# A quantised gated MLP behind attention: the turn back of the scales, two roundings, a kept product and the last gate product moved, and the scale chains cut by one operation

## The chip, the cores and the metric

The kernel runs on one core of one Trainium2 chip. The metric is the device time of one execution in microseconds (us). The core has five engines that work side by side and meet at semaphores: PE (TensorE, matmul; its weight loads are listed apart as PEld), DVE (VectorE), ACT (ScalarE), POOL (GpSimd) and SP (SyncE, which here only issues DMAs). Every engine works through its own list of instructions in order, so an instruction that waits holds back all that stand behind it on that engine.

## The reference, cut to what matters

```python
x = x + tanh(g_xattn) * attention(layernorm(x), ctx, ctx)        # x: 16 x 128 x 512, float32
x = x + tanh(g_ffn)   * ffn(layernorm(x), w_gate, w_up, w_down)

def act_quant(x):                       # per token, 8 bit
    scale = 127.0 / clip(max(abs(x)), EPS)
    return clip(round(x * scale), -128, 127) / scale
def weight_quant(w):                    # ternary
    scale = clip(mean(abs(w)), EPS)
    return clip(round(w / scale), -1, 1) * scale
def h_bitlinear(x, w):
    return act_quant(fwht(x)) @ weight_quant(w).T
def ffn(h, wg, wu, wd):                 # H = 512, I = 2048
    return h_bitlinear(silu(h_bitlinear(h, wg)) * h_bitlinear(h, wu), wd)
```

`fwht` is the normalised Walsh-Hadamard transform along the last axis. Its factors are `C_E` = 512 to the power -1/2 and `C_I` = 2048 to the power -1/2; `QMAX` is 127.

## The kernel before, in words

Attention goes over 16 batches of 128 tokens first; PE sets its pace. The MLP then goes over 4 units (u = 0 to 3) of 4 batches (512 tokens) each. For a unit there are three stages on PE:

- **Gate and up** (`gate_up`): 16 blocks `ob`, each with a gate product (4 matmuls of 128x512 into banks 0 and 2 in turn) and an up product (4 matmuls into banks 1, 3 and 6 in turn). DVE scales the gate product (`gate`, L1391), ACT takes Silu of it (L1091), and DVE multiplies it with the up product (`hidden`, L1396). DVE does `gate(ob)` and then `hidden(ob - 1)`. `gs_done` counts gates, `h_done` hiddens, and PE waits on them before it writes a bank again.
- **Transform** (`transform`): 16 steps that turn the hidden values of the unit, each with 4 float32 matmuls against `had_f` (L863, two entries each in the profile), a copy by ACT (`y_high`), the low part by DVE (`low`, L1371), a second pair of matmuls (L875, L877) and a copy by ACT to `Z`. Between the steps the input of the next unit is normalised, transformed and quantised: `first_turn` (PE, L753), `first_had` (PE, L760), `input_peak` and `input_round` (DVE, L1334 to L1359), for each of its 4 batches tb. The normalised rows come from `front_statistics` (DVE) over `front_scales` (POOL, L517 to L522), `apply` (ACT, L1085) and `front` (POOL, L533 to L540); the rounded rows `q_b` are turned by a DMA into `q1_t`, which the next gate and up reads.
- **Down** (`project`): 4 blocks tb of 16 matmuls (L884). Block tb needs the DMA transposes of pieces 2 tb and 2 tb + 1 of the rounded `Z`, which SP issues in order (`turn`, L344).

The quantisation of a unit u runs beside the gate and up of unit u + 1. DVE takes the maxima of `Z` (`peak`, L1410); PE turns them (L842, after block 4); DVE works out the scales (`chain`, at ob 5, L1417 to L1429); PE turns those back and spreads them (`chain_back`, L849 and L851, after the up product of block 6); DVE copies them out (`chain_end`, at ob 7 behind `hidden(6)`, L1434 to L1438); POOL scales the 8 pieces of `Z` (`scale`, L555); ACT rounds pieces 0 and 1 (`rounding`, L1109 and L1111, after Silu 10 and Silu 12), and DVE the others (L1442): pieces 2, 3, 4 and 5 at ob 12, 13, 14 and 15, pieces 6 and 7 behind the gate and up.

Units 0 and 1 are quantised and projected so in a loop of two rounds: transform(u), gate_up(u + 1), project(u). Then come transform(2), gate_up(3), 11 of the 16 matmuls of the first down block of unit 2 (`project_kept(0, 0, AHEAD)`), transform(3) with no next input, the rest of the down product of unit 2 with the scale chain of unit 3 between its parts, and the down product of unit 3. `mz` is turned at L933 there.

Of the kernel before, what the change touches and what calls it, by code (L numbers as in the profile page):

```python
# [71 lines left out]
def flamingo_block(nc, x, k_t, v, w, gates, ident, had, had16, g_mask, g_mask_t, t_mask, out):  # L72
    with ExitStack() as ctx:
# [138 lines left out]
        AHEAD = 11  # L212
        LAST_PEAKS = {5: 0, 7: 1, 9: 2, 11: 3, 13: 4, 14: 5}
# [17 lines left out]
        ROUND_ACT = {10: 0, 12: 1}  # L231
# [138 lines left out]
        def _(pool):  # L370
# [197 lines left out]
        def _(pe):  # L568
# [238 lines left out]

            def gate_up(u, chain=None, first=False):
                for tb in range(UB):
                    reach(pe, sem(f"q1_in{tb}"), u.times(16, 16))  # L810
                for ob in range(NC):
                    if ob == 1:
                        reach(pe, sem("f_sg"), u.times(UB, UB))
                        if not first:
                            reach(pe, sem("f_su"), u.times(1, 1))
                    if first and ob == 1:
                        weigh(NB - 1, 1)
                        turn_out(NB - 1, 0)
# [9 lines left out]
                    for m, name, banks, used in ((0, "g_done", G_BANKS, "gs_done"), (1, "u_done", U_BANKS, "h_done")):  # L828
                        n = len(banks)
                        if ob >= n:  # L830
                            pe.wait_ge(sem(used), u.times(NC, ob + 1 - n))
                        elif chain is not None and banks[ob] > 5:
                            pe.wait_ge(sem("z_out"), chain.times(16, 16))
                        for j in range(NJ):
                            last = pe.matmul(ps[:, banks[ob % n], :], tern_gu[:, ob // 2, m, j, P * (ob % 2):P * (ob % 2) + P],  # L835
                                             q1_t[:, j, :], start=(j == 0), stop=(j == NJ - 1))
                        last.then_inc(sem(name), 1)
                    if chain is not None and ob == 4:
                        reach_apart(pe, sem("ones_set"),
                                    (sem("mz_done"), chain.times(8, 8)),  # L840
                                    (sem("y_low"), chain.times(16, 16)))
                        pe.transpose(ps[0:NG, 4, 0:P], mz[:, :], ident_f[:, :]).then_inc(sem("c_t1"), 1)  # L842
                    if chain is not None and ob == 6:
                        chain_back(chain)
# [10 lines left out]
            def transform(u, nxt):  # L855

                reach(pe, sem("h_done"), u.times(NC, NC))
                for s in range(18):
# [8 lines left out]
                    if s > 1:  # L867
# [4 lines left out]
                        elif z == 0:  # L872
# [56 lines left out]
            project_kept(0, AHEAD, NC)  # L929
# [240 lines left out]
        def _(dve):  # L1170
# [98 lines left out]
            def early_peak(tb):  # L1269

                dve.wait_ge(sem("f_hc"), tb + 1)
                dve.tensor_reduce(f_max[:, 0:1], had_out, AX_X, ALU.max, apply_absolute_value=True).then_inc(sem("f_c"), 1)
                dve.wait_ge(sem("f_c"), 5 * tb + 1)
                dve.tensor_scalar(f_max[:, 1:2], f_max[:, 0:1], C_E, EPS, ALU.mult, ALU.max).then_inc(sem("f_c"), 1)
                dve.wait_ge(sem("f_c"), 5 * tb + 2)
# [3 lines left out]
                dve.wait_ge(sem("f_c"), 5 * tb + 4)  # L1279
                dve.tensor_scalar(f_max[:, 3:4], f_max[:, 2:3], QMAX * C_E, None, ALU.mult).then_inc(sem("f_c"), 1)  # L1280

            def early_round(tb):

                dve.wait_ge(sem("f_c"), 5 * tb + 5)
                dve.tensor_scalar(q_int, had_out, f_max[:, 3:4], MAGIC, ALU.mult, ALU.add).then_inc(sem("f_qf"), 1)
# [48 lines left out]
            def input_peak(n, bank=1):  # L1334
# [4 lines left out]
                dve.wait_ge(sem("f_c"), n.times(5, 1))  # L1339
                dve.tensor_scalar(f_max[:, 1:2], f_max[:, 0:1], C_E, EPS, ALU.mult, ALU.max).then_inc(sem("f_c"), 1)  # L1340
                dve.wait_ge(sem("f_c"), n.times(5, 2))
                dve.reciprocal(f_max[:, 2:3], f_max[:, 1:2]).then_inc(sem("f_c"), 1)
                dve.tensor_scalar(f_max[:, 4:6], wsc[:, 0:2], f_max[:, 1:2], 1.0 / QMAX, ALU.mult, ALU.mult
                                  ).then_inc(sem("f_c"), 1)
                dve.wait_ge(sem("f_c"), n.times(5, 4))
                dve.tensor_scalar(f_max[:, 3:4], f_max[:, 2:3], QMAX * C_E, None, ALU.mult).then_inc(sem("f_c"), 1)
                dve.wait_ge(sem("f_c"), n.times(5, 5))
                dve.tensor_scalar(q_int, ps[:, bank, :], f_max[:, 3:4], MAGIC, ALU.mult, ALU.add
# [64 lines left out]
            def chain(u):  # L1413
# [52 lines left out]
            def gates_and_chain(u, prev, more=False):  # L1466
                reach(dve, sem("a2_done"), u.times(16))
                for ob in range(NC):
                    gate(u, ob)
                    if ob == 1 and prev is None:  # L1470
                        dve.wait_ge(sem("signed"), 12)
                    if ob > 0:
                        hidden(u, ob - 1)
# [11 lines left out]
                    else:  # L1485
# [4 lines left out]
                        if ob == 7:  # L1490
                            chain_end(prev)
# [117 lines left out]
```

## Time and profile before

| | |
|---|---|
| median of 3 runs | 481.35 us (481.11 to 481.57) |
| the profiled execution | 481.52 us |
| its span, first to last instruction | 479.7 us |
| granted TensorE clock, mean | 1.000 of full speed |
| PE busy | 462.8 us, 96% |
| DVE busy | 392.5 us, 82% |
| ACT busy | 292.8 us, 61% |
| POOL busy | 211.8 us, 44% |

Between the profiled execution and its span lie 1.8 us that are no engine's. A busy share is a mean over stages: a PE that is 96% busy can still wait at a few places, and an engine with a smaller share can be the one that sets a stage. Ends of matmuls are modelled: a matmul is shown with its latency, some 0.16 us beyond the time at which the next one could start.

### The profile page before, as it was taken

Reading aid. Unit: us, or ns where it says so; the run is one execution under the profiler, and the core shown is the slowest. Engines: PE = TensorE matmul, PEld = TensorE weight load, DVE = VectorE, ACT = ScalarE, POOL = GpSimd, SP = SyncE. Lnnn points to the kernel's source line nnn. Section 1 sums busy time; section 2 is a strip of 40 time slices with the busy share of each in tenths; the row PEclk is TensorE's granted clock in tenths of the full one; section 3 lists DMA queues with packets and bytes.
Section 4 is the critical chain, followed back from the end, with each engine's and each line's share of the span. In section 5 each row is a group of like instructions: output and inputs, shape, how many; then the busy total and the mean of one; then the engine's idle time right before and its main releaser. Section 6 shows DMA issues by size and latency. Waiting matters only on the chain.

```text
span 479.7 us, 9075 instructions
## 1 busy us (share of the span) xinstructions
PE 462.8 (96%) x3130; PEld 299.9 (63%) x3130; DVE 392.5 (82%) x765; ACT 292.8 (61%) x465; POOL 211.8 (44%) x314
## 2 busy tenths in 40 slices
PE   8999999999999999989999999999999999989997
PEld 7665656665666434468844479854468874469664
DVE  4889988798968749859997967998885999879892
ACT  3578886677768668877645517653616653648470
POOL 4245455978987544654005834201936200840000
PEclk9999999999999999999999999999999999999999
DMA  6999220021022023000100550100371110153086
GB/s 195 305 348 338 81 53 15 20 57 25 13 66 78 12 56 132 1 1 13 23 11 3 109 138 27 22 11 0 61 158 44 24 23 0 22 88 69 0 134 218
DMA packets 68183, 35.90 MB, mean 75 GB/s; under 512 B 50288, under 2 KB 62960, under 8 KB 68144
## 3 DMA queue, kind: packets, MB, share of 16 engines
q1 hardware_dynamic: 67728, 34.61, 28.2%
q10 hardware_dynamic: 416, 0.79, 0.5%
q8 instruction: 22, 0.36, 0.3%
q14 instruction: 17, 0.14, 0.1%
HBM read 19.26 MB, written 4.19 MB: 49 GB/s over the span
## 4 chain that ended last, share of the span: by engine, by line
PE 63%; DVE 20%; issue 7%; DMA 5%; ACT 3%; SPq 1%; DVEq 0%
PE ps L835 11%; PE ps L884 9%; PE ps L610 9%; PE ps L593 9%; PE ps L636 6%; PE ps L863 5%; DVE y_split L1371 4%; PE ps L653 4%; DVE mz L1410 3%; DVE wst L1391 3%; DMA reg_rest<-reg 2%; PE ps L618 2%; DVE f_max L1337 2%; DVE wst L1396 2%; PE ps L690 1%
## 5 line engine op out<-in xcount | busy, mean ns | idle before, releaser
L835 PE MATMUL ps<-wst 128*128 128x512 bf16 x512 | 112.5, 379 | 0.5 <-DMA wst<-q_b 0.5
L1224 DVE TENSOR_REDUCE reg<-ps 128x4 f32<-128x512 f32 x128 | 82.0, 685 | 25.1 <-PE ps L610 24.3
L555 POOL TENSOR_TENSOR reg_rest<-reg_rest,z_sc 128x1024 f32<-128x1024 f32 x24 | 48.2, 2045 | 92.0 <-DVE z_sc L1434 92.0
L959 ACT ACTIVATE reg<-ps 128x1024 f32<-128x1024 f32 x64 | 65.5, 1023 | 35.7 <-PE ps L618 35.3
L610 PE MATMUL ps<-reg 32*128 32x256 f32 x512 | 86.7, 400 | 0.5 <-DVE reg L1224 0.3
L835 PEld LDWEIGHTS ps<-wst 128*128 128x128 bf16 x512 | 49.5, 98 | 59.6 <-issue 1.8
L593 PE MATMUL ps<-reg 32*128 32x512 f32 x256 | 71.9, 639 | 0.0
L1091 ACT ACTIVATE wst<-wst 128x512 f32<-128x512 f32 x64 | 40.0, 626 | 51.9 <-DVE wst L1391 51.5
L863 PE MATMUL ps<-had_f,wst 128*128 128x128 f32 x512 | 67.1, 275 | 1.3 <-DVE wst L1396 1.3
L863 PEld LDWEIGHTS ps<-had_f,wst 128*128 128x128 f32 x512 | 64.1, 191 | 4.4 <-DVE wst L1396 1.8
L610 PEld LDWEIGHTS ps<-reg 32*128 32x128 f32 x512 | 58.6, 184 | 5.7 <-issue 1.1
L1121 ACT CAST y_split<-ps 128x512 fp32r<-128x512 f32 x64 | 37.3, 586 | 39.6 <-PE ps L863 39.6
L1371 DVE TENSOR_TENSOR y_split<-ps,y_split 128x512 fp32r<-128x512 f32 x64 | 43.5, 684 | 15.0 <-ACT y_split L1121 15.0
L1391 DVE TENSOR_TENSOR wst<-ps,wst 128x512 f32<-128x512 f32 x64 | 43.7, 682 | 10.4 <-PE ps L835 10.4
L884 PE MATMUL ps<-wst,reg_rest 128*128 128x512 bf16 x192 | 42.6, 380 | 3.5 <-DMA reg_rest<-reg 3.5
L1396 DVE TENSOR_TENSOR wst<-ps,wst 128x512 f32<-128x512 f32 x64 | 43.5, 679 | 1.0 <-ACT wst L1091 0.8
L450 POOL TENSOR_TENSOR x_all<-x_all,reg 128x256 f32<-128x256 f32 x32 | 23.8, 745 | 35.8 <-DVE reg L1237 35.8
L1130 ACT COPY reg_rest<-ps 128x512 f32<-128x512 f32 x64 | 37.8, 592 | 2.2 <-PE ps L877 2.1
L884 PEld LDWEIGHTS ps<-wst,reg_rest 128*128 128x128 bf16 x192 | 27.2, 144 | 18.1 <-DMA reg_rest<-reg 2.7
L1410 DVE TENSOR_REDUCE mz<-reg_rest 128x8 f32<-128x1024 f32 (+1 forms) x33 | 38.3, 1171 | 0.0
L636 PE MATMUL ps<-reg 128*32 128x512 f32 x256 | 34.1, 605 | 0.0
L593 PEld LDWEIGHTS ps<-reg 32*128 32x128 f32 x256 | 19.2, 183 | 22.5 <-issue 21.0
(167 smaller groups left out, 747.4 us busy)
## 6 DMA issues: line engine op xcount, KB each, us to landing
wst<-in_w SPq DMA_DIRECT2D x16, 512.0 KB, 8.2
reg<-in_w SPq DMA_DIRECT2D x8, 512.0 KB, 5.4
out<-x_all SPq DMA_DIRECT2D x16, 256.0 KB, 2.1
x_all<-in_x SPq DMA_DIRECT2D x3, 1024.0 KB, 9.9
reg<-in_k_t SPq DMA_DIRECT2D x32, 32.0 KB, 2.3
reg<-in_v SPq DMA_DIRECT2D x4, 256.0 KB, 3.5
x_all<-in_x ACTq DMA_DIRECT2D x1, 512.0 KB, 4.3
reg_rest<-reg SPq DMA_TRANSPOSE x20, 3.2
```

The source lines that it names most:

```text
L593: pe.matmul(ps[:, bank + m, :], kpad[b // CHUNK % 2][strip(i), b % CHUNK, a, :], q_t[b % 4][strip(i), :], start=True, stop=False)
L610: last = pe.matmul(ps[:, row_banks(r) + m, 256 * g:256 * g + 256], q_t[n % 4][strip(i), P * h:P * h + P], kpad[n // CHUNK % 2][strip(i), n ...
L636: last = pe.matmul(O_BANK[SLOT * l:SLOT * l + SLOT, :], v_pad[n // CHUNK % 2][:, n % CHUNK, 4 * kvh + l, :], probs[:, 4 * kvh + l, :], sta ...
L835: last = pe.matmul(ps[:, banks[ob % n], :], tern_gu[:, ob // 2, m, j, P * (ob % 2):P * (ob % 2) + P], q1_t[:, j, :], start=(j == 0), stop= ...
L863: last = pe.matmul(ps[:, Y_BANKS[s % 3], P * k:P * k + P], X[:, 4 * s + k, :, :].rearrange("p c t -> p (c t)"), had_f[:, :], start=True, s ...
L884: last = pe.matmul(ps[:, bank, :], q2.rearrange("p g (t c) -> p c (g t)", c=NC)[:, c, P * tb:P * tb + P], tern_d[:, c, :], start=(c == 0), ...
L959: act.activation(probs[:, 2 * j:2 * j + 2, :], ps[:, bank:bank + 2, :], ACT.Exp, scale=D ** -0.5).then_inc(sem("exp_done"), 1)
L1224: dve.tensor_reduce(neg_max[n % 2][:, g:g + 2, i + m, :], ps[:, row_banks(r) + m, :].rearrange("p (g a t) -> p g a t", g=2, a=2), AX_X, AL ...
L1371: dve.tensor_tensor(y_low[s % RING], ps[:, Y_BANKS[s % 3], :], y_high[s % RING].bitcast(F32), ALU.subtract).then_inc(sem("y_low"), 1)
L1391: dve.tensor_tensor(gs[ob % GS], ps[:, G_BANKS[ob % 2], :], s_row, ALU.mult).then_inc(sem("gs_done"), 1)
L1396: dve.tensor_tensor(X[:, :, ob, :], ps[:, U_BANKS[ob % 3], :].rearrange("p (g t) -> p g t", g=NG), gs[ob % GS].rearrange("p (g t) -> p g t ...
L1410: dve.tensor_reduce(mz[:, g0:g1], Z[:, g0:g1, :], AX_X, ALU.max, apply_absolute_value=True).then_inc(sem("mz_done"), 1)
```

## The change

- In `gate_up` the 8 matmuls of a block are split into a helper `rows`. `chain_back` moves from behind the up product of block 6 to between the gate and the up product of block 7. The gate product of block 15 moves ahead of the up product of block 14: gate 14, gate 15, up 14, up 15. This holds for all four units (`chain_back` for three).
- On DVE `chain_end` moves from behind `hidden(6)` to ahead of it, at ob 7.
- ACT rounds pieces 0 and 1 after Silu 9 and 11 instead of after Silu 10 and 12.
- The input's scale chain (`early_peak`, `input_peak`) loses its last multiplication (L1280, L1346): the factor 1/127 goes into the maximum's scaling, so the reciprocal is the rounding's factor itself. The unit's scale chain (`chain`) loses one too (L1427 and L1429 become one TENSOR_TENSOR with two broadcast operands). The counts of `f_c` and `c_step` go from 5 to 4.
- In the last transform the last 5 matmuls of the first kept down block are issued at step z = 14, between the second matmuls of z = 14 and of z = 15, instead of behind the transform.

```diff
+        KEPT_FILL = {14: (11, 16)}
-        ROUND_ACT = {10: 0, 12: 1}
+        ROUND_ACT = {9: 0, 11: 1}
...
+            def rows(u, chain, ob, m, name, banks, used):
+                n = len(banks)
+                if ob >= n:
+                    pe.wait_ge(sem(used), u.times(NC, ob + 1 - n))
+                elif chain is not None and banks[ob] > 5:
+                    pe.wait_ge(sem("z_out"), chain.times(16, 16))
+                for j in range(NJ):
+                    last = pe.matmul(ps[:, banks[ob % n], :], tern_gu[:, ob // 2, m, j, P * (ob % 2):P * (ob % 2) + P],
+                                     q1_t[:, j, :], start=(j == 0), stop=(j == NJ - 1))
+                last.then_inc(sem(name), 1)
...
+                    if ob < NC - 1:
+                        rows(u, chain, ob, 0, "g_done", G_BANKS, "gs_done")
+                    if chain is not None and ob == 7:
+                        chain_back(chain)
+                    if ob == NC - 2:
+                        rows(u, chain, NC - 1, 0, "g_done", G_BANKS, "gs_done")
+                    rows(u, chain, ob, 1, "u_done", U_BANKS, "h_done")
...
-                    if chain is not None and ob == 6:
-                        chain_back(chain)
...
+                        if nxt is None and z in KEPT_FILL:
+                            project_kept(0, *KEPT_FILL[z])
...
             transform(last_u, None)
-            project_kept(0, AHEAD, NC)
             project_kept(1, 0, 3)
...
-                dve.tensor_scalar(f_max[:, 1:2], f_max[:, 0:1], C_E, EPS, ALU.mult, ALU.max).then_inc(sem("f_c"), 1)
+                dve.tensor_scalar(f_max[:, 1:2], f_max[:, 0:1], 1.0 / QMAX, EPS / (QMAX * C_E), ALU.mult, ALU.max).then_inc(sem("f_c"), 1)
...
-                dve.tensor_scalar(f_max[:, 4:6], wsc[:, 0:2], f_max[:, 1:2], 1.0 / QMAX, ALU.mult, ALU.mult
+                dve.tensor_scalar(f_max[:, 4:6], wsc[:, 0:2], f_max[:, 1:2], C_E, ALU.mult, ALU.mult
                                   ).then_inc(sem("f_c"), 1)
-                dve.wait_ge(sem("f_c"), n.times(5, 4))
-                dve.tensor_scalar(f_max[:, 3:4], f_max[:, 2:3], QMAX * C_E, None, ALU.mult).then_inc(sem("f_c"), 1)
-                dve.wait_ge(sem("f_c"), n.times(5, 5))
-                dve.tensor_scalar(q_int, ps[:, bank, :], f_max[:, 3:4], MAGIC, ALU.mult, ALU.add
+                dve.wait_ge(sem("f_c"), n.times(4, 4))
+                dve.tensor_scalar(q_int, ps[:, bank, :], f_max[:, 2:3], MAGIC, ALU.mult, ALU.add
...
-                dve.tensor_tensor(cz[:, 5, :], cz[:, 3, :], su[:, 1, :], ALU.mult).then_inc(c, 1)
-                dve.wait_ge(c, u.times(5, 5))
-                dve.tensor_scalar(q_sc[:, :, :], cz[:, 5, :].unsqueeze(2).broadcast_to([NG, T8, NC]), QMAX * C_I, None,
-                                  ALU.mult).then_inc(sem("c_qs"), 1)
+                dve.tensor_tensor(q_sc[:, :, :], cz[:, 3, :].unsqueeze(2).broadcast_to([NG, T8, NC]),
+                                  su[:, 1, :].unsqueeze(2).broadcast_to([NG, T8, NC]), ALU.mult).then_inc(sem("c_qs"), 1)
...
                     gate(u, ob)
+                    if prev is not None and ob == 7:
+                        chain_end(prev)
                     if ob > 0:
                         hidden(u, ob - 1)
...
-                        if ob == 7:
-                            chain_end(prev)
```

## Rows read from the trace of the kernel before

**Rows 1.** The page, part 1: busy time and share of each engine.
```profile
PE 462.8 (96%) x3130; PEld 299.9 (63%) x3130; DVE 392.5 (82%) x765; ACT 292.8 (61%) x465; POOL 211.8 (44%) x314
```

**Rows 2.** Who waited for whom: us in total, times, longest.
```profile
PE ps L884 <- DMA reg_rest<-reg: 3.5, 3, 1.7
PE ps L849 <- DVE diag L1429: 1.5, 3, 0.5
```

**Rows 3.** Timeline around `chain_back` in gate_up(1): start, duration, instruction, [idle before].
```profile
252.72 1.03 PE L835 MATMUL ps<-wst 128*128 128x512 bf16 x4
...
253.88 0.22 DVE L1429 TENSOR_SCALAR diag<-cz 64x128 f32<-64x128 f32 x1
254.25 0.24 PE L849 MATMUL ps<-ident_f,diag 64*128 64x64 f32 x1 [0.51 <-DVE diag L1429]
...
257.85 16.23 POOL L555 TENSOR_TENSOR reg_rest<-reg_rest,z_sc 128x1024 f32<-128x1024 f32 x8 [30.65 <-DVE z_sc L1434]
```

**Rows 4.** Timeline of ACT, then the chain that ended last, into project(0).
```profile
262.79 1.13 ACT L1109 ACTIVATE reg_rest<-reg_rest,magics 128x1024 f32<-128x1024 f32 x1
...
267.41 1.16 ACT reg L1111
...
268.58 3.23 DMA reg_rest<-reg
...
271.85 14.04 PE ps L884 x64
```

**Rows 5.** Timeline of DVE, blocks 13 to 15 of gate_up(1) and behind.
```profile
267.63 0.68 DVE L1391 TENSOR_TENSOR wst<-ps,wst 128x512 f32<-128x512 f32 x1
...
273.43 1.19 DVE L1442 TENSOR_SCALAR reg<-reg_rest 128x1024 bf16<-128x1024 f32 x1
...
275.14 1.28 DVE L1442 TENSOR_SCALAR reg<-reg_rest 128x1024 bf16<-128x1024 f32 x2
```

**Rows 6.** Timeline of the next unit's first normalised batch, beside project(0).
```profile
280.75 0.15 DVE L1191 TENSOR_SCALAR ve<-mv 128x1 f32<-128x1 f32 x1
...
285.70 0.73 POOL L540 TENSOR_TENSOR scratch4k<-wst 128x256 f32<-128x256 f32 x1
...
286.62 0.60 PE L753 MATMUL ps<-ident_f,scratch4k 128*128 128x128 f32 x4
```

**Rows 7.** Busy time by stretch, in transform(1).
```profile
298.00:317.00 19.00, 18.29 (x130) 15.75 (x129) 18.54 (x42) 12.93 (x28) 2.84 (x4) 1.00 0.10 21
```

**Rows 8.** Timeline of DVE and POOL, input batches 0 and 3 in transform(1).
```profile
293.75 0.15 DVE L1346 TENSOR_SCALAR f_max<-f_max 128x1 f32<-128x1 f32 x1
...
293.93 0.75 DVE L1348 TENSOR_SCALAR wst<-ps,f_max 128x512 f32<-128x512 f32 x1
...
295.55 0.72 POOL L539 TENSOR_TENSOR scratch4k<-wst 128x256 f32<-128x256 f32 x1 [0.16 <-POOL wst L534]
295.60 0.76 DVE L1358 TENSOR_SCALAR diag<-ident_f,f_max 128x128 f32<-128x128 f32 x1
...
314.37 0.28 DVE L1358 TENSOR_SCALAR diag<-ident_f,f_max 128x128 f32<-128x128 f32 x1
```

**Rows 9.** Timeline at the end of gate_up(0).
```profile
207.43 1.13 ACT L997 ACTIVATE wst<-reg,magics 128x1024 bf16<-128x1024 f32 x1
...
210.03 1.16 PE L863 MATMUL ps<-had_f,wst 128*128 128x128 f32 x8 [1.31 <-DVE wst L1396]
```

**Rows 10.** The chain that ended last and the timeline, end of gate_up(3).
```profile
419.73 3.98 DMA reg_rest<-reg
...
422.88 1.47 DVE L1396 TENSOR_TENSOR wst<-ps,wst 128x512 f32<-128x512 f32 x2
...
423.85 2.57 PE L884 MATMUL ps<-wst,reg_rest 128*128 128x512 bf16 x11 [1.72 <-DMA reg_rest<-reg]
```

**Rows 11.** Timeline at the end of transform(3).
```profile
448.76 0.50 PE L875 MATMUL ps<-y_split,had_r 128*128 128x512 f32 x1 [0.99 <-DVE y_split L1371]
...
451.07 0.11 PEld L933 LDWEIGHTS ps<-ident_f,mz 128*64 128x64 f32 x1 [0.23 <-DVE mz L1410]
```

More of the change, by code:

```diff
@@ L470, in early_scales @@
             def early_scales(tb):
-                pool.wait_ge(sem("f_c"), 5 * tb + 5)
+                pool.wait_ge(sem("f_c"), 4 * tb + 4)
                 reach(pool, sem("f_t2"), tb)
@@ L827, in gate_up @@
                         pe.wait_ge(sem("signed"), ob + 2)
[L828 to L837, printed above, removed]
+                    if ob < NC - 1:
[5 more added lines that the diff above has]
+                    rows(u, chain, ob, 1, "u_done", U_BANKS, "h_done")
                     if chain is not None and ob == 4:
@@ L1272, in early_peak @@
                 dve.tensor_reduce(f_max[:, 0:1], had_out, AX_X, ALU.max, apply_absolute_value=True).then_inc(sem("f_c"), 1)
-                dve.wait_ge(sem("f_c"), 5 * tb + 1)
-                dve.tensor_scalar(f_max[:, 1:2], f_max[:, 0:1], C_E, EPS, ALU.mult, ALU.max).then_inc(sem("f_c"), 1)
-                dve.wait_ge(sem("f_c"), 5 * tb + 2)
+                dve.wait_ge(sem("f_c"), 4 * tb + 1)
+                dve.tensor_scalar(f_max[:, 1:2], f_max[:, 0:1], 1.0 / QMAX, EPS / (QMAX * C_E), ALU.mult, ALU.max).then_inc(sem("f_c"), 1)
+                dve.wait_ge(sem("f_c"), 4 * tb + 2)
                 dve.reciprocal(f_max[:, 2:3], f_max[:, 1:2]).then_inc(sem("f_c"), 1)
-                dve.tensor_scalar(f_max[:, 4:6], wsc[:, 0:2], f_max[:, 1:2], 1.0 / QMAX, ALU.mult, ALU.mult
+                dve.tensor_scalar(f_max[:, 4:6], wsc[:, 0:2], f_max[:, 1:2], C_E, ALU.mult, ALU.mult
                                   ).then_inc(sem("f_c"), 1)
-                dve.wait_ge(sem("f_c"), 5 * tb + 4)
-                dve.tensor_scalar(f_max[:, 3:4], f_max[:, 2:3], QMAX * C_E, None, ALU.mult).then_inc(sem("f_c"), 1)
             def early_round(tb):
-                dve.wait_ge(sem("f_c"), 5 * tb + 5)
-                dve.tensor_scalar(q_int, had_out, f_max[:, 3:4], MAGIC, ALU.mult, ALU.add).then_inc(sem("f_qf"), 1)
+                dve.wait_ge(sem("f_c"), 4 * tb + 4)
+                dve.tensor_scalar(q_int, had_out, f_max[:, 2:3], MAGIC, ALU.mult, ALU.add).then_inc(sem("f_qf"), 1)
             def early_integers(tb):
@@ L1338, in input_peak @@
                                   ).then_inc(sem("f_c"), 1)
-                dve.wait_ge(sem("f_c"), n.times(5, 1))
-                dve.tensor_scalar(f_max[:, 1:2], f_max[:, 0:1], C_E, EPS, ALU.mult, ALU.max).then_inc(sem("f_c"), 1)
-                dve.wait_ge(sem("f_c"), n.times(5, 2))
+                dve.wait_ge(sem("f_c"), n.times(4, 1))
+                dve.tensor_scalar(f_max[:, 1:2], f_max[:, 0:1], 1.0 / QMAX, EPS / (QMAX * C_E), ALU.mult, ALU.max).then_inc(sem("f_c"), 1)
+                dve.wait_ge(sem("f_c"), n.times(4, 2))
                 dve.reciprocal(f_max[:, 2:3], f_max[:, 1:2]).then_inc(sem("f_c"), 1)
-                dve.tensor_scalar(f_max[:, 4:6], wsc[:, 0:2], f_max[:, 1:2], 1.0 / QMAX, ALU.mult, ALU.mult
+                dve.tensor_scalar(f_max[:, 4:6], wsc[:, 0:2], f_max[:, 1:2], C_E, ALU.mult, ALU.mult
                                   ).then_inc(sem("f_c"), 1)
-                dve.wait_ge(sem("f_c"), n.times(5, 4))
-                dve.tensor_scalar(f_max[:, 3:4], f_max[:, 2:3], QMAX * C_E, None, ALU.mult).then_inc(sem("f_c"), 1)
-                dve.wait_ge(sem("f_c"), n.times(5, 5))
-                dve.tensor_scalar(q_int, ps[:, bank, :], f_max[:, 3:4], MAGIC, ALU.mult, ALU.add
+                dve.wait_ge(sem("f_c"), n.times(4, 4))
+                dve.tensor_scalar(q_int, ps[:, bank, :], f_max[:, 2:3], MAGIC, ALU.mult, ALU.add
                                   ).then_inc(sem("f_qf"), 1)
@@ L1418, in chain @@
                                   ).then_inc(c, 1)
-                dve.wait_ge(c, u.times(5, 1))
+                dve.wait_ge(c, u.times(4, 1))
                 dve.tensor_tensor(cz[:, 1, :], cz[:, 0, :], su[:, 1, :], ALU.mult).then_inc(c, 1)
-                dve.wait_ge(c, u.times(5, 2))
-                dve.tensor_scalar(cz[:, 2, :], cz[:, 1, :], C_I, EPS, ALU.mult, ALU.max).then_inc(c, 1)
-                dve.wait_ge(c, u.times(5, 3))
+                dve.wait_ge(c, u.times(4, 2))
+                dve.tensor_scalar(cz[:, 2, :], cz[:, 1, :], 1.0 / QMAX, EPS / (QMAX * C_I), ALU.mult, ALU.max).then_inc(c, 1)
+                dve.wait_ge(c, u.times(4, 3))
                 dve.reciprocal(cz[:, 3, :], cz[:, 2, :]).then_inc(c, 1)
-                dve.tensor_scalar(cz[:, 4, :], cz[:, 2, :], wsd_tg[0:NG, :], None, ALU.mult).then_inc(sem("c_qs"), 1)
-                dve.wait_ge(c, u.times(5, 4))
-                dve.tensor_tensor(cz[:, 5, :], cz[:, 3, :], su[:, 1, :], ALU.mult).then_inc(c, 1)
-                dve.wait_ge(c, u.times(5, 5))
-                dve.tensor_scalar(q_sc[:, :, :], cz[:, 5, :].unsqueeze(2).broadcast_to([NG, T8, NC]), QMAX * C_I, None,
-                                  ALU.mult).then_inc(sem("c_qs"), 1)
+                dve.tensor_scalar(cz[:, 4, :], cz[:, 2, :], wsd_tg[0:NG, :], QMAX * C_I, ALU.mult, ALU.mult
+                                  ).then_inc(sem("c_qs"), 1)
+                dve.wait_ge(c, u.times(4, 4))
+                dve.tensor_tensor(q_sc[:, :, :], cz[:, 3, :].unsqueeze(2).broadcast_to([NG, T8, NC]),
+                                  su[:, 1, :].unsqueeze(2).broadcast_to([NG, T8, NC]), ALU.mult).then_inc(sem("c_qs"), 1)
             def chain_end(u, f_tok=f_tok):
```

## The prediction

> **What bounds the kernel now.** I read the page's shares first: PE is busy 96% of the span, so what can be won is PE's idle time and whatever makes a stage longer than PE's own work [rows 1]. The list of waits says where PE stood idle for others: three times for the DMA that turns the rounded values, in front of a down product, 3.5 us in all (one of 1.7, two of 0.9), and three times 0.5 us for the scales that `chain_back` turns [rows 2]. Then I went through the timeline stage by stage. Attention is PE work on both sides and the change touches nothing on its path. Gate and up is PE-bound except at `chain_back`. A transform with a next input is DVE's: between 298 and 317 us DVE is busy 18.54 of 19 us, and PE's matmuls wait in small pieces for it [rows 7]. Transform(3) is PE's, with a tail that DVE sets.
>
> **chain_back between gate 7 and up 7.** The last 4 matmuls of up 6 start at 252.72, follow each other at 0.22 us (64 down matmuls take 14.04 us) and leave PE free at 253.58; the turn back starts at 254.25, right behind DVE's last chain operation, done at 254.10 [rows 3, 4]. So PE loses 0.67 us (0.51 in the list, which counts from the modelled end). With gate 7 (4 x 0.22 = 0.87 us) in front, PE comes to the turn back at 254.45, after the scales. Cost 0, gain 0.67 in each of three units. No row shows the new TENSOR_TENSOR with two broadcast operands over 128 elements: below it cannot be under the 0.22 of the operation that it replaces, above it is under the 0.74 of an L1396 with 512 elements [rows 3, 10]. I take about 0.3, nearer to the 0.22 since it has the same 128 elements. One operation of 0.18 less stands in front of it, so the scales come at about 254.0, or at 254.45 by the upper end: both are in time for PE.
>
> `chain_end` no longer waits behind `hidden(6)`. The spread scales are ready about 1.1 us of `chain_back` after 254.45, and DVE is then just past `gate(7)`. I put the copy at 255.65 and POOL's first block at 255.85 instead of 257.85, 2.0 us earlier; it ends its 16.2 us at 272.1 instead of 274.1 [rows 3].
>
> **Roundings after Silu 9 and 11.** PE's down product waits for piece 1: rounded by ACT until 268.57, landed 3.23 us later, PE starts at 271.85, 1.03 us after it could (0.87 in the list) [rows 4]. One block of gate and up is 8 x 0.22 = 1.73 us. With the pair of roundings (1.13 + 1.16 us) one block earlier and PE's 0.67 us, piece 1 is done about 2.3 us earlier, at 266.3, and lands at 269.5; PE is ready at 270.15. POOL's second block is done by 260, so the roundings don't wait for it. Silu 10 stands behind the first rounding and ends 0.2 us after `hidden(10)` would like it; DVE has 0.4 us to spare in each block there. The wait goes entirely: 1.03 us in each loop round.
>
> What is late next? Pieces 2 to 7 are rounded by DVE, which runs without a gap from block 12 on, and moves by PE's 0.67 only. Piece 5 is the tightest: rounded from 273.43 for 1.19 us beside POOL, while pieces 6 and 7, with POOL done, take 0.64 each [rows 5]. New, POOL ends at 272.1 and piece 5 starts at 272.8, so it should take 0.65 and end at 273.4, landing at 276.7; block 2 of the down product wants it at 270.15 + 32 x 0.22 = 277.1. In time by 0.4.
>
> But PE is then 1.70 us early at `first_turn`, and its rows come over another path: statistics on DVE (end 280.90), POOL, ACT, POOL's L540 (end 286.43), against PE's L753 at 286.62 [rows 6]. That path moves by DVE's 0.67 + 0.53 and has about 0.1 to spare. So PE waits 0.4 us at L753, and a loop round brings 1.3 us, not 1.7. Two rounds: 2.6 us.
>
> **Gate 15 ahead of up 14.** In gate_up(0), transform(0) waits 1.31 us for the last hidden [rows 9]. Gate 15 comes 0.87 us earlier, but ACT stands in front of Silu 15 with a weight sign operation from 207.43 to 208.56, and Silu 15 started at 208.62 already. Gain 0.1; if ACT were free it would be 0.5. In the other units PE now wants bank 2 at 268.2 in old time, and `gate(13)` frees it at 268.31 [rows 5]: a wait of 0.1, which in the loop is lost in the wait at L753.
>
> **The last unit.** The same 0.67, and PE's wait for piece 1 is 1.72 us, 1.88 from the last possible start; the landing took 3.98 us there [rows 10]. New it lands at 417.3 + 3.98 = 421.3, just when PE is ready. The 11 matmuls then end 2.5 us earlier. Transform(3) also needs `hidden(15)`, done at 424.35 in old time and 0.67 earlier now, 423.7, against PE at 423.8. Gain 2.4 us, which passes whole through the PE-bound transform(3).
>
> **Shorter input chain.** L1346 to L1348 is 0.18 us from start to start [rows 8], 12 times in the three DVE-bound transforms: 2.2 us if all of it counts. For input batches 0 and 1 I count nothing: DVE's next scalar operations run beside POOL's four operations of the following batch and end with them, L1358 takes 0.76 us against POOL's L539, and 0.28 where POOL is idle [rows 8]. POOL's times come from PE's `first_turn` and don't move with the chain. Batches 2 and 3 have no such neighbour: 2 x 0.18 = 0.4 a transform, 1.1 us in all, and the ends are 0 and 2.2. The Trainium skill (SBUF — State Buffer, "Who interferes with whom") says that a two-port tensor_scalar on DVE and a GpSimd operation exclude each other for the whole instruction; by that rule batches 0 and 1 give 0, and the trace agrees with L1358's 0.76 against 0.28 us. The same section speaks against the new TENSOR_TENSOR, whose two SBUF inputs would wait behind a reading POOL; here POOL has been idle for 30.65 us, so it costs nothing.
>
> **Kept product into transform(3).** Between the second matmuls of z = 14 and z = 15 PE has a hole of 1.2 us (0.99 in the list) before 448.76; 5 x 0.22 = 1.1 fill it. What follows is L933 at 451.07, which waits for DVE's maxima, not for PE [rows 11]. The time that the 5 matmuls leave behind becomes idle in front of L933. Gain 0, loss at most 1.1. The shorter unit chain brings nothing there either, since 9 kept matmuls lie between the two turns.
>
> **Sum.** 0.1 + 2.6 + 1.1 + 2.4 = 6.2 us from the 481.5 of the profiled execution, 475.3; the median of the runs is 0.15 lower, so 475.2.
>
> **Rivals.**
> - The input chain counts in full: DVE is nearly always busy in these transforms, but the neighbouring POOL work speaks against it. 1.1 us more, 474.1. Chance 0.14.
> - The input chain counts for nothing, because the DMA turn of `q_b` or ACT sets the end of the transform: 476.3. Against it stands DVE's saturation. Chance 0.10.
> - Piece 5 stays at 1.19 us beside POOL. Then the statistics move 0.53 less and PE waits that much longer at L753, twice: 476.3; with a landing of 3.98 instead of 3.23 us block 2 of the down product waits as well and it is 476.9. Chance 0.15. The rule of the Trainium skill on the shared port (SBUF — State Buffer, "Who interferes with whom") is on the other side: with POOL done before piece 5 starts, nothing holds it.
> - No change within 0.2%: the waits at the down product all come back at the next pieces, L753 and the last unit's `hidden(15)`, and only the turn back remains, under 1 us. Chance 0.03.
> - Slower: the roundings, now in front of Silu 10 and 11, hold `hidden(10)` and with it `gate(12)`, `gate(13)` and PE at gate 15, where the order of this change leaves no slack. The whole pair (2.3 us) passed on, less DVE's 0.4 of spare time, is 1.9 us, twice in three units, 11.4 us against 6.2: 486.7. It decides from 1.0 us per rounding on. Before the change the same two roundings stood in front of Silu 11 and 13 and held nothing. Chance 0.02.
>
> The forecast itself has 0.56, with 474.6 to 476.0 as its own range. The bounds of the terms (0 to 0.5; 1.3 to 3.4; 0 to 2.2; 0.7 to 2.5) would reach from 472.8 to 479.5; I cut to 473.6 to 477.2. A difference under 0.2% (1 us) is about what a measurement can't tell from none. Faster 0.95, same 0.03, slower 0.02.
>
> **What would show it.** L849 with no idle before it, three times; POOL's L555 some 2 us earlier against PE's L849; the first L884 of each down product directly behind L835; L753 with an idle of about 0.4 behind project; L1442 of piece 5 at 0.65 us; L863 still waiting over 1 us after gate_up(0); idle in front of L933 longer, the stretch from L933 to the end unchanged at 28.6 us. The prediction is wrong if PE waits at gate 15, or at later blocks of the down product.

## The result and the profile after

| | median | range | runs |
|---|---|---|---|
| before | 481.46 us | 481.11 to 481.59 | 4 |
| after | 476.32 us | 475.92 to 476.53 | 4 |

The ratio is 0.9893 (95% interval 0.9878 to 0.9909), 5.1 us faster. The forecast was 475.2 us, made of 6.2 us of gain. The profiled execution of after took 475.92 us, its span is 474.1 us, the granted TensorE clock 1.000.

The page of after, part 1, and below it the list of waits (us in total, times, longest):

```profile
PE 459.7 (97%) x3110; PEld 299.1 (63%) x3130; DVE 390.8 (82%) x745; ACT 293.0 (62%) x465; POOL 211.3 (45%) x314
```

```profile
PE ps L817 <- DVE wst L1396: 2.1, 3, 0.7
PE ps L761 <- DVE wst L1353: 1.2, 3, 0.4
PE ps L871 <- DVE wst L1401: 1.1, 1, 1.1
PE ps L942 <- DVE mz L1415: 0.9, 1, 0.9
...
PE ps L754 <- POOL scratch4k L541: 0.2, 1, 0.2
```

Both entries of [rows 2] are gone: no DMA wait in front of a down product, none in front of the turn back (L857 now). In their place a new one stands on top: L817 is the gate and up product, L1396 is `gate`. Three times 0.7 us, once in each of the units 1 to 3, PE waits for a gate product's bank. The forecast had 0.1 there.

The timeline of after in gate_up(1), start, duration, instruction, [idle before], the same stretch as [rows 3, 4, 5]; L556 is `scale` on POOL, L1446 `rounding` on DVE, L894 the down product:

```profile
252.22 0.28 DVE L1433 TENSOR_TENSOR diag<-cz,su 64x128 f32<-64x128 f32 x1
...
252.87 0.27 PE L857 MATMUL ps<-ident_f,diag 64*128 64x64 f32 x1
...
254.51 15.78 POOL L556 TENSOR_TENSOR reg_rest<-reg_rest,z_sc 128x1024 f32<-128x1024 f32 x8 [28.22 <-DVE z_sc L1438]
...
263.78 1.89 POOL L556 TENSOR_TENSOR reg_rest<-reg_rest,z_sc 128x1024 f32<-128x1024 f32 x1
...
263.97 2.26 DVE L1446 TENSOR_SCALAR reg<-reg_rest 128x1024 bf16<-128x1024 f32 x1
266.15 0.68 DVE L1396 TENSOR_TENSOR wst<-ps,wst 128x512 f32<-128x512 f32 x1
...
266.88 2.76 PE L817 MATMUL ps<-wst 128*128 128x512 bf16 x12 [0.70 <-DVE wst L1396]
267.35 1.18 DVE L1446 TENSOR_SCALAR reg<-reg_rest 128x1024 bf16<-128x1024 f32 x1
...
269.48 6.86 PE L894 MATMUL ps<-wst,reg_rest 128*128 128x512 bf16 x30
...
271.95 0.68 DVE L1446 TENSOR_SCALAR reg<-reg_rest 128x1024 bf16<-128x1024 f32 x1
```

Read it from below. PE's idle of 0.70 us ends with `gate(13)`, which DVE starts at 266.15 because piece 2's rounding held it for 2.26 us. That rounding starts 0.19 us behind the start of a POOL block. Up to there the blocks follow each other at 1.86 us; the next one starts at 265.64, and 1.67 us of waiting and 0.6 of work make the 2.26. Before, the same rounding had started 1.01 us into its block and took 1.44, a row that the forecast never looked at. These two rows of before show it:

```profile
265.26 1.89 POOL L555 TENSOR_TENSOR reg_rest<-reg_rest,z_sc 128x1024 f32<-128x1024 f32 x1
...
266.27 1.44 DVE L1442 TENSOR_SCALAR reg<-reg_rest 128x1024 bf16<-128x1024 f32 x1
```

Where the 5.6 us between the two spans come from, by the start of the same instruction on both sides. For the transforms the mark at their end is DVE's first `gate`, since PE's first row there can lack a matmul record (0.21 us).

| stage | measured | forecast |
|---|---|---|
| launch to the third batch of attention | -0.34 | not counted; 55.00 to 56.05 us in the 14 profiled kernels |
| attention from there (input chain of unit 0) | -0.61 | 0 |
| gate_up(0) | -0.13 | -0.1 |
| three transforms with a next input (0.40, 0.45, 0.47) | -1.32 | -1.1 |
| two loop rounds of gate and up and down (0.57, 0.66) | -1.23 | -2.6 |
| gate_up(3) to the end | -1.96 | -2.4 |

The rest of the rows that answer to those of before, all from the timeline of after: the end of gate_up(0) [rows 9], the next unit's first turn [rows 6], input batch 0 in transform(1) [rows 8], the end of gate_up(3) [rows 10], and the end of transform(3) [rows 11].

```profile
206.52 1.13 ACT L1006 ACTIVATE wst<-reg,magics 128x1024 bf16<-128x1024 f32 x1
...
208.95 1.16 PE L871 MATMUL ps<-had_f,wst 128*128 128x128 f32 x8 [1.14 <-DVE wst L1401]
...
284.57 0.65 PE L754 MATMUL ps<-ident_f,scratch4k 128*128 128x128 f32 x4 [0.22 <-POOL scratch4k L541]
...
291.49 0.21 DVE L1350 TENSOR_SCALAR f_max<-wsc,f_max 128x2 f32<-128x2 f32 x1
...
291.74 0.75 DVE L1353 TENSOR_SCALAR wst<-ps,f_max 128x512 f32<-128x512 f32 x1
...
412.95 2.26 DVE L1446 TENSOR_SCALAR reg<-reg_rest 128x1024 bf16<-128x1024 f32 x1
...
415.87 2.76 PE L817 MATMUL ps<-wst 128*128 128x512 bf16 x12 [0.70 <-DVE wst L1396]
...
418.47 2.54 PE L894 MATMUL ps<-wst,reg_rest 128*128 128x512 bf16 x11
...
442.50 1.03 PE L894 MATMUL ps<-wst,reg_rest 128*128 128x512 bf16 x4
...
443.37 0.50 PE L883 MATMUL ps<-y_split,had_r 128*128 128x512 f32 x1
...
445.68 0.30 PE L942 MATMUL ps<-ident_f,mz 128*64 128x128 f32 x1 [0.87 <-DVE mz L1415]
```

The operation between L1350 and L1353 is gone. In unit 3 the 11 kept matmuls follow without the 1.72 us for the DMA, but behind the same 0.70 at gate 15. Transform(3) has kept matmuls in its hole (four of the five have a record) and pays in front of L942 (0.87 us of idle, 0.23 in [rows 11]); and from there to the end it is 28.4 us, 28.6 before.

### The profile page after: what moved, and what is told of

Read it like the earlier page. It is cut to its first block, busy times and chain, and to the rows that moved or that the text cites. A ratio compares the mean times of both kernels' runs of the same rounds, so it can differ in the third digit from the quotient of the medians.

```text
span 474.1 us, 8995 instructions
## 1 busy us (share of the span) xinstructions
PE 459.7 (97%) x3110; PEld 299.1 (63%) x3130; DVE 390.8 (82%) x745; ACT 293.0 (62%) x465; POOL 211.3 (45%) x314
## 4 chain that ended last, share of the span: by engine, by line
PE 73%; DVE 13%; issue 7%; ACT 3%; POOL 2%; DMA 1%; DVEq 0%; POOLq 0%; ACTq 0%
PE ps L817 14%; PE ps L611 10%; PE ps L594 9%; PE ps L871 9%; PE ps L637 7%; PE ps L894 6%; PE ps L654 4%; PE ps L883 2%; PE ps L885 2%; PE ps L761 2%; DVE wst L1401 2%; PE ps L619 2%; PE ps L691 2%; DVE y_split L1376 2%; DVE st L1196 1%
## 5 line engine op out<-in xcount | busy, mean ns | idle before, releaser
L817 PE MATMUL ps<-wst 128*128 128x512 bf16 x499 | 111.7, 379 | 3.3 <-DVE wst L1396 2.1
L817 PEld LDWEIGHTS ps<-wst 128*128 128x128 bf16 x512 | 49.1, 98 | 62.1 <-DVE wst L1396 4.2
L556 POOL TENSOR_TENSOR reg_rest<-reg_rest,z_sc 128x1024 f32<-128x1024 f32 x24 | 47.3, 2009 | 84.7 <-DVE z_sc L1438 84.7
L1396 DVE TENSOR_TENSOR wst<-ps,wst 128x512 f32<-128x512 f32 x64 | 43.5, 680 | 8.2 <-PE ps L817 8.2
L894 PE MATMUL ps<-wst,reg_rest 128*128 128x512 bf16 x186 | 42.2, 380 | 0.4
L894 PEld LDWEIGHTS ps<-wst,reg_rest 128*128 128x128 bf16 x192 | 27.4, 145 | 13.9 <-issue 0.6
```

The lines of the kernel that those rows point to most:

```text
L556: pool.tensor_tensor(z, z, sc, ALU.mult).then_inc(sem("z_scaled"), 1)
L894: last = pe.matmul(ps[:, bank, :], q2.rearrange("p g (t c) -> p c (g t)", c=NC)[:, c, P * tb:P * tb + P], tern_d[:, c, :], start=(c == 0), ...
L1396: dve.tensor_tensor(gs[ob % GS], ps[:, G_BANKS[ob % 2], :], s_row, ALU.mult).then_inc(sem("gs_done"), 1)
```

## The experiments

All ran beside the kernel before (medians 481.35 to 481.62 in the four groups). The times below are medians with their ratio to it; after's own is 476.32 (0.9893). The edits are made in the kernel after.

**The input chains long again.**

```diff
-                dve.tensor_scalar(f_max[:, 1:2], f_max[:, 0:1], 1.0 / QMAX, EPS / (QMAX * C_E), ALU.mult, ALU.max).then_inc(sem("f_c"), 1)
+                dve.tensor_scalar(f_max[:, 1:2], f_max[:, 0:1], C_E, EPS, ALU.mult, ALU.max).then_inc(sem("f_c"), 1)
...
+                dve.tensor_scalar(f_max[:, 3:4], f_max[:, 2:3], QMAX * C_E, None, ALU.mult).then_inc(sem("f_c"), 1)
```

> The changed kernel with the fifth operation of the input's scale chain back, in attention (4 times) and in the three transforms (12 times). Reading of the two traces: attention lengthens by 0.14 us a batch, 0.55 us, each transform by 0.4 us, 1.2 us together: 477.9 to 478.3 us. Rival (the difference of the attention stages is that of two executions): 477.3 to 477.6 us. If all 12 count: 479.0 us.

478.80 us (478.60 to 479.03), 0.9943 [0.9929, 0.9956]: 2.5 us more than after. By the marks used above, attention from its third batch gives back 0.60 us, and the three transforms 0.40, 0.41 and 0.51; they are then as long as before's within 0.04. So the chain is worth 1.3 us in the transforms, the size that the forecast gave it, and 0.6 in attention, which it had put at nothing: four operations of 0.18 us are 0.72. The other 0.5 us of the 2.5 lies in neither. In the profiled execution the launch is 0.47 us longer than after's, and gate_up(3) to the end 0.69 (0.30 of it a wait for a DMA in the last down product); that these have to do with the chain is not shown.

**Gate 15 ahead in unit 0 only.**

```diff
-                    if ob < NC - 1:
+                    if ob < NC - 1 or not first:
                         rows(u, chain, ob, 0, "g_done", G_BANKS, "gs_done")
...
-                    if ob == NC - 2:
+                    if ob == NC - 2 and first:
```

> The changed kernel with gate 15 ahead of up 14 in the first unit only. In the changed kernel PE waits 0.70 us at gate 15 in each of units 1 to 3. Theory A (shared port: DVE rounds piece 2 in 2.26 us because it waits out a POOL block that began 0.19 us before it, and gate(13) comes late): these three waits go, since the old order wants gate(13) 0.87 us later; DVE's own times stay (2.26 us), so in the loop the 0.7 us is mostly lost again at the next first_turn, and only the last unit keeps it: 475.3 to 475.9 us. Theory B (gate 15 ahead is harmless, the time went elsewhere): 476.3 us, no change.

476.44 us (476.27 to 476.56), 0.9895 [0.988, 0.991]: no change, a miss for the expectation of 475.3 to 475.9. The order of the two products decides where PE waits, not how long the kernel takes. Piece 2 takes 2.27 us as in after; PE no longer waits at gate 15, but for what that lateness reaches next. Timeline of this kernel, round 1 and unit 3:

```profile
264.18 2.27 DVE L1446 TENSOR_SCALAR reg<-reg_rest 128x1024 bf16<-128x1024 f32 x1
...
276.13 7.12 PE L894 MATMUL ps<-wst,reg_rest 128*128 128x512 bf16 x31 [0.22 <-DMA reg_rest<-reg]
...
284.80 0.65 PE L754 MATMUL ps<-ident_f,scratch4k 128*128 128x128 f32 x4 [0.66 <-POOL scratch4k L541]
...
418.47 2.59 PE L894 MATMUL ps<-wst,reg_rest 128*128 128x512 bf16 x11 [0.40 <-DVE wst L1396]
```

**The two roundings of ACT back behind Silu 10 and 12.**

```diff
-        ROUND_ACT = {9: 0, 11: 1}
+        ROUND_ACT = {10: 0, 12: 1}
```

> The changed kernel with ACT's roundings after Silu 10 and 12 again. Theory A (shared port): piece 2 on DVE still takes about 2.26 us and PE still waits 0.7 us at gate 15, because POOL and DVE stand to each other as before; the down product waits for piece 1 by about 0.1 us in the loop and 0.9 us in the last unit, 477.0 to 477.6 us. Rival C (the moved roundings hold Silu 10 and 11 and so DVE and gate 15): piece 2 falls back to 1.4 us and the waits at gate 15 go; what is lost at piece 1 is won there, 476.0 to 476.6 us.

476.87 us (476.67 to 477.67), 0.9907 [0.9892, 0.9922]. Piece 2 takes 2.18 us and PE's waits at gate 15 stay, so the moved roundings don't make them:

```profile
264.44 2.18 DVE L1446 TENSOR_SCALAR reg<-reg_rest 128x1024 bf16<-128x1024 f32 x1
...
267.28 2.76 PE L817 MATMUL ps<-wst 128*128 128x512 bf16 x12 [0.71 <-DVE wst L1396]
```

A loop round is as long as after's, 43.23 us: with DVE late, the earlier piece 1 is worth nothing in the loop. In the last unit it is worth 0.26 us, the time by which transform(3) now starts later against the unit's first `gate`. Another 0.27 us lies behind the turn of `mz`, where nothing was changed and the kernels' profiles differ by up to 0.4 us among themselves (28.42 to 28.80).

**The turn back in its old place.**

```diff
-                    if chain is not None and ob == 7:
-                        chain_back(chain)
...
+                    if chain is not None and ob == 6:
+                        chain_back(chain)
```

> The changed kernel with the turn back behind up 6 again (the copy of the scales stays ahead of hidden 6). Theory A (shared port): PE loses 0.6 us at the turn back in three units again, but POOL's blocks begin about 1.4 us later against DVE, piece 2 then waits only 0.3 us for the port and takes about 1.0 us, and the three waits of 0.7 us at gate 15 go: 475.9 to 476.8 us, nearly no change. Rival D (the turn back's move simply gives 0.67 us a unit and the port has nothing to do with it): 478.3 us.

475.96 us (475.79 to 476.05), 0.9885 [0.987, 0.99]: no slower than after, a little faster if anything. The waits of [rows 2] in front of the turn back are back (0.57, 0.58, 0.56 us at L857); but POOL's first block now starts 14.31 us behind the unit's first `gate` instead of 13.17, the rounding 23.24 instead of 22.63, piece 2 takes 0.93 us, and no wait is left at gate 15. What one move gives, the other takes.

**POOL 0.6 us later, by the copy behind hidden(6) again.** The turn back stays in its new place.

```diff
-                    if prev is not None and ob == 7:
-                        chain_end(prev)
                     if ob > 0:
                         hidden(u, ob - 1)
+                    if prev is not None and ob == 7:
+                        chain_end(prev)
```

> The changed kernel with DVE's copy of the scales behind hidden(6) again: everything that depends on it, POOL's eight blocks first, begins 0.6 us LATER. Theory A (shared port): piece 2's rounding then meets the end of a POOL block after 0.45 us instead of 1.67 us and takes about 1.05 us instead of 2.26; the 0.7 us waits at gate 15 go; 473.6 to 474.6 us, faster by about 2 us. Rival E (an earlier start of POOL is a gain or nothing): 476.3 to 477.0 us.

474.97 us (474.38 to 475.52), 0.9869 [0.9854, 0.9884], 1.35 us faster than after. Nothing is done sooner here, one copy is done later:

```profile
255.84 16.24 POOL L556 TENSOR_TENSOR reg_rest<-reg_rest,z_sc 128x1024 f32<-128x1024 f32 x8 [28.80 <-DVE z_sc L1438]
264.72 0.99 DVE L1446 TENSOR_SCALAR reg<-reg_rest 128x1024 bf16<-128x1024 f32 x1
```

The rounding starts 8.88 us behind POOL's first block, 0.40 before the sixth starts (5 x 1.855 = 9.28), and takes 0.40 + 0.6. The list of waits has no L817 for L1396.

**The same aim by moving DVE's operation.** Piece 2 is rounded ahead of `hidden(11)` instead of behind it.

```diff
+                    if prev is not None and ob == 12:
+                        rounding(prev, 2)
                     if ob > 0:
                         hidden(u, ob - 1)
...
-                    if 12 <= ob < 14:
+                    if ob == 13:
```

> The changed kernel with DVE's rounding of piece 2 ahead of hidden(11) instead of behind it, 0.6 us earlier against POOL, whose start stays. Theory A (shared port): it waits 0.4 us and takes about 1.0 us; the waits at gate 15 go; 473.6 to 474.6 us. Rival E (DVE has the same work in either order): 476.3 us.

473.99 us (473.03 to 474.59), 0.9842 [0.9829, 0.9855]: 2.3 us under after. POOL keeps its early start and piece 2 takes 0.99 us. The last experiment below comes to the same time, with useless work in it; the loop rounds are the shortest here. So of all versions this is the one to keep.

**ACT rounds piece 2 as well** (after Silu 13), and DVE one less.

```diff
-        ROUND_ACT = {9: 0, 11: 1}
+        ROUND_ACT = {9: 0, 11: 1, 13: 2}
...
-                        if 12 <= ob < 14:
+                        if ob == 13:
```

> The changed kernel with piece 2 rounded by ACT (behind Silu 13) instead of DVE, POOL's start as in the changed kernel. Theory A (shared port): gate(13) follows hidden(11) at once and PE never waits at gate 15; piece 3, DVE's first, meets POOL instead and may wait up to a block, but behind gate(13), where PE has slack: 474.3 to 475.5 us. Rival (ACT, with three roundings, holds Silu 14 and 15): 476.3 us or slower.

475.55 us (475.34 to 475.57), 0.9871 [0.9853, 0.9888]. The wait at gate 15 is gone and a loop round is 0.4 us shorter than after's, but piece 3 now starts just behind the start of the seventh block and takes 2.31 us. ACT ends piece 2 at 268.51, DVE piece 3 at 268.53; SP issues their transposes one behind the other, at 268.54 and 269.81, the second lands at 273.16, and the down product waits for it:

```profile
266.22 2.31 DVE L1446 TENSOR_SCALAR reg<-reg_rest 128x1024 bf16<-128x1024 f32 x1
...
273.20 3.03 PE L894 MATMUL ps<-wst,reg_rest 128*128 128x512 bf16 x13 [0.54 <-DMA reg_rest<-reg]
```

**No kept matmuls in transform(3).**

```diff
-                        if nxt is None and z in KEPT_FILL:
+                        if False:
...
+            project_kept(0, AHEAD, NC)
```

> The changed kernel with the 5 kept matmuls behind transform(3) again. Both readings of the tail: what follows waits for DVE's maxima, so 476.3 us, no change; L942 then stands behind 8 matmuls instead of 3 and waits under 0.1 us instead of 0.87. If the fill had cost or brought its 1.1 us, 475.2 or 477.4 us.

476.59 us (476.50 to 476.60), 0.9898 [0.9883, 0.9913]. The hole before L883 is back (0.99 us), the wait in front of the turn of `mz` is gone, and gate_up(3) to the end is 0.18 us longer than after's, 0.11 of it ahead of the turn of `mz`: the fill is worth 0.1 to 0.2 us.

**POOL later by idle work of its own.** Three additions of 64x2 elements on POOL (0.49 us in all, into a row that nobody reads; their results are unused in this kernel and the next three) between POOL's wait for the scales and its first block.

```diff
                 reach(pool, sem("c_sc"), u.times(1, 1))
+                for k in range(3):
+                    pool.tensor_tensor(cz[:, 5, 2 * k:2 * k + 2], ones_f[0:NG, 0:2], ones_f[0:NG, 2:4], ALU.add).then_inc(sem("spare_done"), 1)
```

> The changed kernel with three added small POOL operations (64x2 elements each, results unused) between POOL's wait for the scales and its first block, on three units: 0.4 to 0.7 us of useless work that delays POOL and touches nothing else. Theory A (shared port): piece 2 takes 0.9 to 1.2 us instead of 2.26, the waits at gate 15 go, 473.6 to 474.6 us. Rival E: 476.3 us or slower.

494.29 us (493.70 to 495.08), 1.0265 [1.0251, 1.0279]. A miss by 20 us: the theory that only the phase counts (where in a POOL block DVE's operation starts) is not enough. Its timeline (`gate` is L1398 here, the rounding L1448, `scale` L558), and its busy time by stretch (length, PE, PEld, DVE, ACT, POOL busy with counts, granted clock, DMA share, GB/s):

```profile
262.69 7.45 POOL L558 TENSOR_TENSOR reg_rest<-reg_rest,z_sc 128x1024 f32<-128x1024 f32 x4
...
264.30 6.40 DVE L1448 TENSOR_SCALAR reg<-reg_rest 128x1024 bf16<-128x1024 f32 x1
...
271.35 4.87 PE L819 MATMUL ps<-wst 128*128 128x512 bf16 x11 [4.84 <-DVE wst L1398]
```

```profile
265.00:271.30 6.30, 1.51 (x7) 0.49 (x5) 6.30 (x3) 0.46 (x1) 5.14 (x3) 0.89 0.22 42
271.30:276.00 4.70, 4.65 (x11) 1.64 (x12) 4.54 (x8) 1.89 (x3) 0.00 (x0) 0.50 0.69 133
```

DVE doesn't come in at the end of the running block. POOL's last four go through back to back, 4 x 1.86 = 7.45 us, to 270.14, and only then does the rounding do its 0.6. PE idles 4.84 us; after that the granted clock is 0.50 over 4.7 us, the 1.2 GHz level, and a matmul takes 0.43 us instead of 0.22. Three times 4.84 against three times 0.70 us of wait are 12.4 of the 18 us that it costs against after. The rest, 5.6, is of the size of the halved clock: behind the three idles PE works on at 0.50 for 5.35, 2.80 and 5.08 us, and half of that, 6.6 us, is an upper estimate of its cost.

**Two, and five, such operations** (the five of 64x1 elements), to tell the phase from the operations themselves.

> The changed kernel with two added small POOL operations in place of the three of the run before, which made piece 2 take 6.40 us. POOL starts 0.3 us later than in the changed kernel, and a POOL block ends about 0.1 us after DVE comes to piece 2 (0.25 us with three). Plain lock (DVE gets the port at the next block's end): piece 2 takes 0.7 us, 473 to 474 us. If a DVE operation that comes shortly before a block's end misses it and then all that follow: about 6.5 us again, 493 to 496 us. If it is the presence of added operations: 6.4 us as well, which the run with five tells apart.

> The same with five added small POOL operations: a POOL block ends about 0.55 us after DVE comes to piece 2. If the place in time decides: piece 2 takes 1.15 us, no wait at gate 15, 474.0 to 475.2 us, although POOL does more and starts later than in the run at 494 us. If the presence of added operations decides: 6 us, about 494 us.

494.36 us (494.13 to 494.66), 1.0261 [1.0242, 1.0279], and 496.00 us (495.64 to 496.23), 1.0294 [1.0275, 1.0312]. Piece 2 takes 6.26 and 6.69 us, again until POOL's last block is done. With two, three and five operations the rounding starts 9.16, 9.03 and 8.74 us behind POOL's first block: three phases, one picture, so it is not the phase.

**The three operations with a wait for them** ahead of the first block.

```diff
+                reach(pool, sem("spare_done"), u.times(3, 3))
```

> The changed kernel with the three added small POOL operations that led to 494 us, and behind them a wait of POOL for their own completion, so that the first of the eight blocks follows a wait again, as in the changed kernel. If DVE is shut out because the blocks stand in POOL's queue behind operations without a wait: piece 2 takes 0.7 to 1.2 us and the time is 473.6 to 475.0 us. If the added operations as such (or POOL's code) decide: piece 2 takes over 6 us and the time is 493 to 495 us.

474.04 us (473.94 to 474.72), 0.9846 [0.983, 0.9863]. Timeline:

```profile
254.92 0.49 POOL L554 TENSOR_TENSOR cz<-ones_f 64x2 f32<-64x2 f32 x3 [28.22 <-DVE z_sc L1441]
255.48 16.24 POOL L559 TENSOR_TENSOR reg_rest<-reg_rest,z_sc 128x1024 f32<-128x1024 f32 x8
...
264.38 0.97 DVE L1449 TENSOR_SCALAR reg<-reg_rest 128x1024 bf16<-128x1024 f32 x1
```

The same useless half microsecond, and the kernel is 2.3 us faster than after instead of 18 us slower: with the wait in front, DVE gets in at the end of a block again, and the later phase pays. The rounding starts 8.90 us behind the first block, between the 8.74 and the 9.03 at which it was shut out, so the wait makes the difference and not the place in time.

## Why the prediction was nearly right, and what it missed

The start of the first rounding that DVE does beside POOL (piece 2; piece 3 where ACT takes piece 2), counted from the start of POOL's first block in gate_up(1), sorts the kernels whose first block directly follows a wait. Blocks begin at multiples of 1.855 us, so at 9.28 and 11.13:

| kernel | starts after | takes | rule: to the next block, + 0.6 |
|---|---|---|---|
| before | 8.42 | 1.44 | 1.46 |
| copy behind hidden(6) | 8.88 | 0.99 | 1.00 |
| piece 2 before hidden(11) | 8.88 | 0.99 | 1.00 |
| three operations and a wait | 8.90 | 0.97 | 0.98 |
| turn back at 6 | 8.93 | 0.93 | 0.95 |
| after | 9.46 | 2.26 | 2.27 |
| gate 15 in unit 0 only | 9.45 | 2.27 | 2.28 |
| roundings back | 9.53 | 2.18 | 2.20 |
| ACT takes piece 2 | 11.27 | 2.31 | 2.31 |

The Trainium skill (SBUF — State Buffer, "Who interferes with whom") says that a 2-port tensor_scalar on DVE and a GpSimd instruction exclude each other for the whole instruction, and that the one issued first holds the other up; in these nine kernels the trace agrees to 0.02 us (the two that are not listed, input chains long and no kept matmuls, fit as well: 2.08 and 2.27). It does not account for the 6.40 us behind the unwaited operations.

**The step that failed** is the sentence on the last gate: PE wants bank 2 and `gate(13)` frees it "a wait of 0.1". It moved POOL by 2.0 us (measured 1.86 against the unit's first `gate`: 15.03 us behind it before, 13.17 after) and DVE by 0.67, and used the relative shift for piece 5 alone, which fell to 0.68 as forecast. It never applied it to piece 2, whose 1.44 us it carried over. Counted from the unit's first `gate`, piece 2 came 0.82 us earlier (23.45 to 22.63) and POOL 1.86, so it fell 1.04 us later in POOL's series, across a block boundary: 1.44 became 2.26 us, `gate(13)` late, and PE waits 0.70 us in three units. It had named what would show this: "The prediction is wrong if PE waits at gate 15". The cause is shown from both sides: with POOL later (three ways) or DVE's rounding earlier the waits go; with neither (the roundings back, gate 15 ahead in unit 0 only) piece 2 still takes over 2.1 us and the time stays.

**The loop rounds, -2.6 forecast, -1.23 measured.** The terms themselves hold where the phase is right. From DVE's first gate to the next first turn a round takes 43.80 us before, 43.23 and 43.14 after, but 42.49 and 42.39 with the copy behind `hidden(6)` and 42.46 and 42.37 with the three operations and a wait: -1.3 to -1.4 each, the forecast 1.3. With piece 2 ahead of `hidden(11)` it is 41.99 and 41.96, -1.8, more than forecast: DVE is earlier still, and no wait is left at the next unit's first turn. The limit at the next unit's first turn was seen rightly: PE waits 0.22 us there in round 1 of after and 0.35 with the copy behind `hidden(6)`, 0.4 forecast.

**The last unit, -2.4 forecast, -1.96 measured**, short by the same wait; it is -2.8 with the copy behind `hidden(6)`. The DMA waits of [rows 2, 10] are gone as said.

**The input chain** came out right in size (-1.32 against -1.1; measured by putting it back, 1.3), but in part by luck: it is not batches 2 and 3 that bring it. Counted from the unit's first turn in transform(1), DVE leads the kernel before by 0.05 us at the maximum of batch 1, 0.26 at that of batch 2, 0.45 at that of batch 3 and 0.63 at batch 3's `diag`, and by 0.45 at the next unit's first `gate`. So batch 0 brings nothing, as forecast; batch 1, counted as nothing, brings 0.2, batch 2 its 0.2; and batch 3's is lost again, since the first row of the next unit (314.56) then starts behind PE's own matmuls and no longer behind the DMA of `q_b`, landed at 314.21. Batch 1's 0.2 is the phase once more, in a row that the forecast took to be fixed. Before, first, and after, behind it:

```profile
302.11 0.73 POOL L540 TENSOR_TENSOR scratch4k<-wst 128x256 f32<-128x256 f32 x1
302.17 0.95 DVE L1357 TENSOR_SCALAR q_b<-wst 128x512 bf16<-128x512 f32 x1
...
299.87 0.47 DVE L1362 TENSOR_SCALAR q_b<-wst 128x512 bf16<-128x512 f32 x1
300.01 0.91 POOL L541 TENSOR_TENSOR scratch4k<-wst 128x256 f32<-128x256 f32 x1
```

Before, DVE's operation starts 0.06 us behind POOL's and takes 0.95; after, it starts 0.14 ahead of POOL's and takes 0.47, and POOL's takes 0.91 instead of 0.73. The rival that all 12 count, 1.1 us more, did not come: the undone chain gives 0.4 to 0.5 us a transform. **Attention** was wrong: "the change touches nothing on its path". `early_peak` is in the change, and its four operations are worth 0.6 us before gate_up(0). This 0.6 hid part of the shortfall, so by luck the total came out closer than its terms: without it the gain would have been some 4.5 us (an estimate, 5.1 less 0.6), not 6.2.

**Gate 15 in unit 0** gave 0.13 (0.1 forecast), ACT's weight sign operation in front of Silu 15 being the limit. **The fill** gave 0.1 to 0.2, put at 0. **The slower rival** had the right place, PE at gate 15 without slack, but the wrong engine: ACT's roundings (which now stand in front of Silu 10 and 12, not 10 and 11 as it has it) hold nothing there, putting them back leaves PE's three waits at gate 15 as they are.

## What to carry to other kernels

Where DVE and POOL exclude each other, price an operation by where it falls in the other engine's series, not by its old duration: here a start 0.3 to 0.4 us ahead of a block's end cost 0.93 to 0.99 us and one 0.2 us behind it 2.27. After every shift of one of the two, go through each such operation again, the ones ahead of the tight one too; and if one falls badly, move it by one place rather than give up the shift (473.99 us against 476.32). Keep slack at the place that the late operation feeds before an order is tightened there.

## What the runs showed of the hardware

- A DVE tensor_scalar that waits for POOL is not always served when the running POOL instruction ends. With two, three or five small POOL operations directly ahead of the eight blocks and no wait between, it stood until all eight were done (6.26, 6.40 and 6.69 us, three times a kernel alike); with a semaphore wait of POOL ahead of the first block, in the same kernel, it got in at the next boundary (0.97 us). Why the wait makes the difference is open: the blocks are the same in both, and nothing here looks into the arbitration.
- The lock works both ways: a POOL block at whose start DVE's rounding holds it off shows 2.34 us instead of 1.89 (in after the seventh and eighth, before the sixth to eighth). In the kernels where DVE was shut out all eight take 1.89.
- Idle time of PE cost twice where it was long: with three idles of 4.84 us the granted clock was 0.50 for 6.8, 3.4 and 6.8 us, from 1.5, 0.6 and 1.8 us before the idle's end on. Around the waits of 0.70 us of after it stayed at 1.00.
